# Mode index outside, channel and real/imaginary part innermost, in a spectral mixing stage

## The reference

```python
# layer 0
x_freq = rfft2(gn(x))                          # (16, 64, 256, 129)
xf = x_freq.reshape(16, 4, 16, 256, 129)       # 4 heads of 16 channels
core = einsum('bhixy,hioxy->bhoxy', xf[..., :32, :17], weight)   # complex, one 16x16 matrix per head and mode
x = x + irfft2(pad(core)) + bias
# layer 1
x = x + lorentz_norm(gn(x))                    # per pixel, over the 64 channels
```

## Time and profile before

| what | value |
|---|---|
| median of 3 runs | 4943.81 us (4943.03 to 4945.26) |
| span of the profiled execution | 4939.4 us |
| busy: PE, DVE, ACT, POOL | 3805.1, 3399.5, 2240.3, 1460.1 us |
| stage A, first load to last result of DVE | 0 to about 1347 us |
| DVE's sums over the channels (L391) | 502.7 us in 256 instructions |

### The profile page before, as it was taken

How to read it: one execution, slowest core, us unless ns; L and a number is a source line. 1 busy time by engine, 2 the same in 40 slices (tenths; PEclk the granted TensorE clock), 3 DMA queues, 4 the chain that set the end, 5 groups by cost and what they waited for, 6 DMA issues and landing times.

```text
span 4939.4 us, 72319 instructions
## 1 busy us (share of the span) xinstructions
PE 3805.1 (77%) x23619; PEld 2097.6 (42%) x23874; DVE 3399.5 (69%) x3499; ACT 2240.3 (45%) x3020; POOL 1460.1 (30%) x737
## 2 busy tenths in 40 slices
PE   7777777777144344433999999999999999999998
PEld 3444444444111011002555555555555555555554
DVE  2989889898863433343776677667767776676677
ACT  5555555455022233232554455445554554454544
POOL 0010110101100010001454444444444444444444
PEclk9988888898566677766999999999999999999999
DMA  9565756655099989982777777777777777777776
GB/s 367 192 251 188 258 198 229 228 193 213 14 381 357 364 342 363 351 345 81 224 235 219 227 239 221 224 223 241 224 222 224 237 227 224 227 234 224 223 244 217
DMA packets 288845, 1197.47 MB, mean 242 GB/s; under 512 B 30174, under 2 KB 46846, under 8 KB 205828
## 3 DMA queue, kind: packets, MB, share of 16 engines
q1 hardware_dynamic: 274740, 1151.85, 68.7%
q0 software_dynamic: 11600, 38.32, 2.1%
q10 hardware_dynamic: 2304, 4.20, 0.2%
HBM read 883.32 MB, written 310.94 MB: 242 GB/s over the span
## 4 chain that ended last, share of the span: by engine, by line
PE 50%; issue 3%; DMA 1%; DVE 0%; SPq 0%; POOL 0%; ACT 0%; POOLq 0%; ACTq 0%
PE c_p_u L1129 20%; PE c_p_z L1099 11%; PE c_p_t L1112 10%; PE c_p_p L1153 5%; PE c_p_g L1135 4%; DMA c_mv<-bmap 0%; POOL c_ot L1306 0%; ACT c_zc L1189 0%; DVE c_zc L1280 0%; DMA c_ys<-spec 0%; SPq L1070 0%; DMA c_x<-x 0%; DVE c_rt L1288 0%; SPq L1069 0%; PE c_p_z L1174 0%
## 5 line engine op out<-in xcount | busy, mean ns | idle before, releaser
L1306 POOL TENSOR_TENSOR c_ot<-c_s,c_u 128x1024 f32<-128x1024 f32 x512 | 1211.3, 2366 | 1411.6 <-DVE c_s L1259 1411.6
L1189 ACT ACTIVATE c_zc<-c_p_z 34x512 f32<-34x512 f32 x512 | 546.4, 1067 | 1316.0 <-PE c_p_z L1099 1261.5
L1250 DVE TENSOR_TENSOR c_u<-c_xt,c_p_u 128x1024 f32<-128x1024 f32 x512 | 625.3, 1221 | 745.0 <-PE c_p_u L1129 722.5
L1129 PE MATMUL c_p_u<-c_mv,c_zc 128*128 128x256 f32 x4096 | 1043.7, 399 | 76.5 <-issue 75.5
L1129 PEld LDWEIGHTS c_p_u<-c_mv,c_zc 128*128 128x128 f32 x4096 | 750.7, 193 | 590.1 <-issue 465.7
L650 PE MATMUL b_p_al<-b_xt,b_awc 128*32 128x512 f32 x2048 | 333.9, 791 | 502.6 <-ACT b_al_r L692 314.9
L1259 DVE SCALAR_TENSOR_TENSOR c_s<-c_u,keep_k,c_p_g 128x1024 f32<-128x1024 f32 x512 | 655.8, 1281 | 18.0
L1269 DVE TENSOR_TENSOR c_ot<-c_ot,c_p_p 128x1024 f32<-128x1024 f32 x512 | 621.4, 1214 | 1.8 <-POOL c_ot L1306 1.3
L1218 ACT ACTIVATE c_sq<-c_s,c_btcol 128x1024 f32<-128x1024 f32 x512 | 589.2, 1151 | 52.8 <-DVE c_s L1259 22.3
L1099 PEld LDWEIGHTS c_p_z<-c_idft_h,c_ys 128*34 128x34 f32 x8176 | 477.6, 113 | 224.7 <-issue 215.2
L1099 PE MATMUL c_p_z<-c_idft_h,c_ys 128*34 128x64 f32 x8176 | 559.6, 222 | 7.8 <-ACT c_zc L1189 7.8
(11 more groups left out here) (177 smaller groups left out, 3090.8 us busy)
## 6 DMA issues: line engine op xcount, KB each, us to landing
a_xt<-in_x SPq DMA_DIRECT2D x256, 1024.0 KB, 9.7
b_xt<-in_x SPq DMA_DIRECT2D x128, 2048.0 KB, 18.9
c_xt<-in_x SPq DMA_DIRECT2D x256, 1024.0 KB, 6.4
out<-c_ot SPq DMA_DIRECT2D x256, 1024.0 KB, 8.5
maps<-b_maps POOLq DMA_DIRECT2D x16, 768.0 KB, 14.9
c_rt<-maps SPq DMA_DIRECT2D x256, 48.0 KB
a_wm<-in_wmix SPq DMA_DIRECT2D x1, 8704.0 KB, 34.9
b_spt<-spec POOLq DMA_DIRECT2D x32, 272.0 KB, 23.4
```

The costliest lines, as they stand in the source:

```text
L1129: ins = nc.tensor.matmul(p_u[:, W * r:W * r + W], zc[ck % 2][:, (t % TCH) * ROWS + row], mv[t % 2][:, W * row:W * row + W], start=True, st ...
L1189: S.activation(zc[chunk_buffer][0:M2, :, 16 * part:16 * part + 16].rearrange("m h c -> m c h"), p_z[0:M2, :].rearrange("m (c h) -> m c h", ...
L1250: V.tensor_tensor(u[n][:], xt[t % 4][:, 1024 * n:1024 * n + 1024], p_u[:], ALU.add).then_inc(u_done, 1)
L1306: P.tensor_tensor(ot[t % 4][:, 1024 * n:1024 * n + 1024], s0[n][:], u[n][:], ALU.add).then_inc(v_done, 1)
```

## The change

The 32 numbers of a mode are laid next to each other. The weights are transposed on the host so that each (output channel, row) has ky outside and (channel, part) inside. `xh` gets the same order, so the products come out in it, and L391 reads the products in address order. `xm`, `xk`, `y` and everything that is stored keep their layout. L460, which makes `xh`, still reads in address order, but now writes in steps of 32 elements (128 bytes); it multiplies the same 544 numbers. L465 and the one-time change of sign of the weights (L478) touch every second element. No instruction is added, removed or moved on any engine.

```diff
@@ stage_a
-        xh = sb("xh", [128, CI, M2])
+        xh = sb("xh", [128, KY, 2 * CI])
@@ mix
-    ch.inc(V.tensor_tensor(prod[o % 2][:], wm[:, o], xh[:].rearrange("p i m -> p (i m)").unsqueeze(1).to_broadcast((128, 2, CI * M2)), ALU.mult))
+    ch.inc(V.tensor_tensor(prod[o % 2][:], wm[:, o], xh[:].rearrange("p k n -> p (k n)").unsqueeze(1).to_broadcast((128, 2, CI * M2)), ALU.mult))
@@ mix
-    ch.inc(V.tensor_reduce(y[:, o].rearrange("p (a k) -> p a k", a=2), prod[o % 2][:].rearrange("p a (n k) -> p a k n", k=KY), AX_X, ALU.add))
+    ch.inc(V.tensor_reduce(y[:, o].rearrange("p (a k) -> p a k", a=2), prod[o % 2][:].rearrange("p a (k n) -> p a k n", k=KY), AX_X, ALU.add))
@@ start
-    ch.inc(V.tensor_tensor(xh[:].rearrange("p (g i) m -> p g (i m)", i=2), xk[:].rearrange("p (g i) m -> p g (i m)", i=2),
-                           row(22, 8).unsqueeze(2).to_broadcast((128, 8, 2 * M2)), ALU.mult))
+    ch.inc(V.tensor_tensor(xh[:].rearrange("p k (g j) -> p g j k", j=4), xk[:].rearrange("p i m -> p (i m)").rearrange("p (g j k) -> p g j k", j=4, k=KY),
+                           row(22, 8).unsqueeze(2).unsqueeze(3).to_broadcast((128, 8, 4, KY)), ALU.mult))
@@ start
-    dcs = pair(xh[:, :, 0])
+    dcs = pair(xh[:, 0, 0::2])
@@ before the loop, once
-    neg = wm[:, :, 0].rearrange("p o (i r k) -> p o i r k", r=2, k=KY)[:, :, :, 1]
+    neg = wm[:, :, 0].rearrange("p o (n r) -> p o n r", r=2)[:, :, :, 1]
@@ arrays_of, on the host
-    wmix = np.stack([np.stack([re, im], 4), np.stack([im, re], 4)], 3)
+    wmix = np.stack([np.stack([re, im], 4), np.stack([im, re], 4)], 3).transpose(0, 1, 2, 3, 6, 4, 5)
```

## The result

The changed kernel takes 4755.02 us (median of 4 runs, 4749.65 to 4757.91) against 4943.42 us (4 runs); the ratio is 0.9621, with a 95% interval of 0.9607 to 0.9634. The forecast was 4760 us, range 4749 to 4812.

The account below looks back on a forecast made before the run. DVE was taken to pace stage A's mixing slots; 4943.8 us less 184.3 us for L391 (128 pairs, 1.44 us each) plus 0.4 us for L460 gave 4759.9 us, range 4749 to 4812.

Parts of the forecast that it names:

- DVE paces the slots: Stage A's mixing slots: DVE is busy 60.56 of 62.50 us and sets their pace; 128 x 1.44 = 184.3 us saved.
- L391 at 1286 ns: The sum over channels, 256 instructions, falls from 2005 to 1286 ns each when it reads in address order.
- The argument from 21 and 53 ns a result: L391 and L807 both make 34 results but differ in excess per result, so excess goes with elements read in steps.
- L460 at +0.4 us, covered by L434's wait: Scattered write in `start`: 0.4 us more, hidden behind DVE's 4.3 us wait for POOL except in the first image.
- L386, L465, L478 at nothing: The product L386 and the two instructions stepping by two elements were to change the time by nothing.
- PE keeps up: Mixing slots: PE's free slot of 6.46 us against DVE's new 6.53, modes delivered about 1.4 us ahead.
- PE's wait for L405: End of an image's slots: PE's wait for the energy sum was to shrink from 7.63 to some 3.7 us.
- only a part of the sum's excess goes: Rival: something besides the step, beside PE and ACT, holds half of L391's excess; gain 92 us, 4852 us, chance 0.05.
- PE takes over: Rival: in the slots the low clock lasts one slot longer, 71 us lost over 14 images, 4831 us, chance 0.12.
- The period: Time between two `finish` in stage A: forecast to fall from 78.42 to 66.9 us.

Follow-up runs that it names:

- sum_only: The kernel before with only L391 reading in address order; weights, xh and L460 keep their old layout (wrong sums): 4758.15 us, ratio to before 0.9631.
- steps: The changed kernel with L391 reading in a different step in each of eight slots, L401 and L402 writing in steps (wrong sums): 4887.68 us, one run.
- write_only: The changed kernel with L391 reading in the old step of 17 elements (wrong sums): 4944.38 us, ratio to before 1.0005.
- mean_late: The changed kernel with mean_sum, whose L434 waits for POOL, moved behind the next image's second mixing slot: 4697.28 us, ratio to before 0.9508.
- mean_late_flat: mean_late with L460 writing xh in address order again (wrong products): 4691.02 us, ratio to before 0.9492.
- half_sum: The changed kernel with L391 summing only the first 16 of a mode's 32 numbers: 4666.00 us, ratio to before 0.9443.

## Why the prediction was right

The mechanism was the one forecast, and 4760 us was 5 us above the measurement, less than the 8 us between the fastest and the slowest of its runs; the span was forecast at 4755.5 and is 4756.3 us. By its steps:

- *DVE paces the slots.* Shown: stage A's mixings gave 184.8 us against 184.3 forecast, and sum_only gives the same with one instruction's pattern.
- *L391 at 1286 ns.* Measured 1281. That the excess goes with the step and not with the 34 results is shown by steps: at 34 sums, address order takes 1281 ns and step 17 2011 ns; at 32 sums, steps 1 and 2 take 1281 ns and step 4 2157 ns. The argument from 21 and 53 ns a result was right in kind; its 0.66 and 0.82 ns an element are two points of an uneven set and no slope.
- *L460 at +0.4 us, covered by L434's wait.* Measured +0.39 us; the cover is shown from both sides, by write_only (there, and free) and by the pair mean_late and mean_late_flat (uncovered, and paid).
- *L386, L465, L478 at nothing.* L386 stayed; L465 became 14 ns shorter, which is the excess that the prediction had read in it.
- *PE keeps up.* It did, with more reserve than worked out. I took PE's pieces after its longest stall at their old durations and let row transform 5 end 31.4 us after `finish`; it ended at 30.3 (586.44 + 3.65 - 559.78). The column transform took 2.78 instead of 3.62 us, because TensorE ran less of this stretch at its lower level: the granted clock was 0.72 in the 6.2 us from the end of the longest stall, where it was 0.52. In the changed kernel:

```profile
582.00:588.20 6.20, 6.19 (x32) 4.94 (x34) 5.98 (x7) 0.00 (x0) 0.00 (x0) 0.72 1.05 386
```

In finer slices, the clock was at its lower level from about 662.6 to 672.8 us before, 2.2 us after PE had run out of work, and in the changed kernel only from 582.0 to 585.5 us, from PE's restart on. The stall was shorter (5.34 against 6.49 us), but no run shows that this is the cause. PE's wait for L405 was 5.3 us in the mean (69.1 / 13) against 3.7 forecast; the 1.1 us of the row transform and five slots that are 0.06 us shorter account for 1.4 of the 1.6 us.
- *The rival "only a part of the sum's excess goes"* could be judged from the trace of before. In the last mixing PE and ACT are idle and the DMA engines too (0.00 busy from 1282 to 1333 us), and a pair of L391 still takes 3.85 us, against 4.00 us in a slot beside them:

```profile
1284.84 3.85 DVE L391 TENSOR_REDUCE a_y<-a_prod 128x34 f32<-128x1088 f32 x2
```

So the company has at most 0.15 us of the 1.5 us that a pair lost.
- *The rival "PE takes over"* did not happen here, but half_sum shows that the tie was real: take a further microsecond off DVE's slot, and PE sets the pace.
- *The period* of 66.9 us was measured at 67.0; the slot of 6.53 us at 6.54.

What stays open is why step 24 costs 1.33 ns an element, and why the steps are uneven at all, and what moved TensorE's clock. I varied the step and the number of sums, not where the products lie.

## What to carry to other kernels

Where an instruction of VectorE takes markedly longer than an instruction over as many elements in address order, look at its innermost step before its kind: here a sum over channels took 57% longer for its access pattern (2005 against 1281 ns). If one of producer and consumer has to step far, let it be the smaller one (544 elements once an image against 1088 elements sixteen times), best beside a wait that is there anyway. And before counting such a gain in full, work out the free pace of the engine behind: here it stood 2% behind, enough for this change and not for the next one in the slots. A saving in the tail still came through in full: mean_late's period fell by the whole 4.0 us.

## What the runs showed of the hardware that I had not expected

- fp32 of VectorE in steps of 16 bytes is as dear as, or dearer than, steps of 64 bytes (2157 against 1993 ns for 1088 elements); in steps of 8 bytes it is free (1281 ns).
- A step of 96 bytes costs more than any other one tried, nearly twice the extra of 48 or 128 bytes (2719 ns for 1080 elements, against 2069 for 1080 and 2044 for 1088), and 2710 ns also with the other engines idle.
- Strided writes cost about what strided reads do (0.67 to 0.75 ns an element), and are free in steps of 8 bytes (720 ns for 544 elements).
- A strided read takes a few per cent longer beside the other engines and the loads than alone (step of 68 bytes: median 2008 against 1965 ns in the kernel before); in address order it doesn't (median 1282 ns in both, in the changed kernel).
